# Graph-attention kernel on one Trainium2 core: a new schedule for the counting stage

## The reference

```python
x = x + gat(layernorm(x))             # 8 heads of 64
# per head h:
Wx = x @ Ws[h] + Wb[h]
s  = leaky_relu(Wx[dst] @ a_w[h,:64] + Wx[src] @ a_w[h,64:] + a_b[h], 0.2)
alpha = segment_softmax(s, dst)
out_h = segment_sum(alpha[:, None] * Wx[src], dst)
# then: a mixture of 16 experts (one chosen for all nodes), a graph
# convolution over the same edges with self loops, a mixture of 8 experts per node
```

## Time and profile before

| what | value |
|---|---|
| median of 3 runs | 553.72 us (551.4 to 556.36) |
| the profiled execution | 548.52 us, span 546.8 us |
| merge of pair 159, the last (end of the counting) | at 135.21 us of the span |
| TensorE busy over the span | 487.1 us (89%) |
| VectorE busy | 437.4 us (80%) |
| ScalarE busy | 343.9 us (63%) |
| GpSimd busy | 69.6 us (13%) |

### The profile page before, as it was taken

How to read it: one execution, slowest core, us unless ns; L and a number is a source line. 1 busy time by engine, 2 the same in 40 slices (tenths; PEclk the granted TensorE clock), 3 DMA queues, 4 the chain that set the end, 5 groups by cost and what they waited for, 6 DMA issues and landing times.

```text
span 546.8 us, 11526 instructions
## 1 busy us (share of the span) xinstructions
PE 487.1 (89%) x4388; PEld 356.0 (65%) x4389; DVE 437.4 (80%) x908; ACT 343.9 (63%) x659; POOL 69.6 (13%) x85
## 2 busy tenths in 40 slices
PE   0979999986689999999899889988899999999995
PEld 0756666664688888888677644544466587776662
DVE  8767777664999999995898778995787787887871
ACT  5366666657899999984665643344444558856820
POOL 3000000000000000000000020123334420321232
PEclk9989999998799999999999999999999999999998
DMA  6970000002011111102000069000001118966111
GB/s 153 354 258 1 1 2 1 2 2 100 2 50 50 50 50 49 50 4 78 1 1 0 2 221 337 1 0 2 3 21 42 59 60 298 373 237 215 62 54 54
DMA packets 25253, 45.11 MB, mean 82 GB/s; under 512 B 6962, under 2 KB 6998, under 8 KB 25197
## 3 DMA queue, kind: packets, MB, share of 16 engines
q1 hardware_dynamic: 23212, 39.16, 21.0%
q0 software_dynamic: 1952, 5.18, 2.6%
q10 hardware_dynamic: 32, 0.01, 0.0%
HBM read 33.23 MB, written 11.95 MB: 83 GB/s over the span
## 4 chain that ended last, share of the span: by engine, by line
PE 52%; DVE 33%; issue 8%; ACT 4%; DMA 2%; POOL 1%; ACTq 0%; SPq 0%; POOLq 0%; DVEq 0%
PE bank L1442 8%; PE bank L1832 6%; PE bank L1708 6%; DVE work L1125 4%; PE bank L1516 4%; PE bank L1468 4%; PE bank L1509 4%; PE bank L1803 3%; PE bank L1420 3%; PE bank L1611 3%; PE bank L1624 3%; DVE rings L1125 2%; DVE big L1235 2%; DVE st L887 2%; DVE work L1030 1%
## 5 line engine op out<-in xcount | busy, mean ns | idle before, releaser
L1611 PE MATMUL bank<-big,work 128*128 128x130 f16 x1080 | 67.4, 224 | 8.4 <-DVE work L1125 8.4
L1611 PEld LDWEIGHTS bank<-big,work 128*128 128x128 f16 x1080 | 64.3, 100 | 10.4 <-DVE work L1125 4.9
L1509 PE MATMUL bank<-big 128*128 128x180 f16 x320 | 58.1, 267 | 4.2 <-DVE big L988 4.2
L988 DVE TENSOR_TENSOR big<-mid 128x1024 f16<-128x1024 f16 (+1 forms) x88 | 59.8, 734 | 0.1
L685 ACT ACTIVATE mid<-aux,small 128x1280 f16<-128x1280 f32 x36 | 47.3, 1349 | 0.7 <-DVE work L1125 0.3
L1624 PE MATMUL bank<-big,mid 128*128 128x260 f16 x400 | 47.1, 275 | 0.1
L1708 PE MATMUL bank<-mid 128*128 128x512 f16 x200 | 47.2, 378 | 0.0
L586 ACT ACTIVATE mid<-bank 128x180 f32 x80 | 26.5, 331 | 28.9 <-PE bank L1516 28.1
L1624 PEld LDWEIGHTS bank<-big,mid 128*128 128x128 f16 x400 | 38.2, 96 | 7.5 <-issue 0.3
L1468 PE MATMUL bank<-big,rings 128*128 128x512 f16 x120 | 42.7, 378 | 0.1
L1509 PEld LDWEIGHTS bank<-big 128*128 128x128 f16 x320 | 35.6, 118 | 8.8 <-DVE big L988 5.9
(11 more groups left out here) (325 smaller groups left out, 1126.3 us busy)
## 6 DMA issues: line engine op xcount, KB each, us to landing
big<-in_L_ffn_W SPq DMA_DIRECT2D x10, 1024.0 KB, 9.0
mid<-in_L_ffn_W SPq DMA_DIRECT2D x6, 1024.0 KB, 14.4
xperm_scratch<-work SPq DMA_DIRECT2D x1, 5753.0 KB, 20.3
aux<-thr_scratch SPq DMA_DIRECT2D x8, 640.0 KB, 3.8
aux<-xperm_scratch SPq DMA_DIRECT2D x8, 523.0 KB, 4.3
row<-in_x SPq DMA_DIRECT2D x1, 2304.0 KB
aux<-in_L_gnn_Ws SPq DMA_DIRECT2D x4, 256.0 KB, 4.6
work<-in_L_gnn_W SPq DMA_DIRECT2D x1, 1024.0 KB, 6.6
```

The costliest lines, as they stand in the source:

```text
L988: return V.tensor_tensor(out.rearrange("p c (v two) -> p c v two", two=2), values.rearrange("p (v two) -> p v two", two=2).unsqueeze(1).to ...
L1509: mm(count_bank(base, k)[:, 0:RW], L_ring[:, slot, k * CH + j, :], R_ring[:, slot, k * CH + j, :], start=j == 0, stop=False)
L1611: ins = mm(acc_region(h, t), weighted[i % NC][:, t * P:(t + 1) * P], VP[:, s, part, h, :, :].rearrange("p b f -> p (b f)"), start=False, s ...
```

## The change

The schedule constants are new: 12 pairs a tile, first linear piece at pair 16, one piece a pair. The zeroing of C and C2 is split into halves: VectorE and ScalarE do one each, GpSimd two. The targets load before the sources, under semaphores of their own; four tiles of x load before the other six; the zero fill of a scratch tensor waits until all of x is there. The eight products on zeros are gone, all four W0 transposes come ahead of the tables' wait, ScalarE rounds W0 ahead of the pairs, tile 0's statistics stand in `pair_tables`. `scores` stands ahead of the last batch, `exponents` inside it, the threshold rows are copied by VectorE behind it, into another buffer.

```diff
-WARM = 8
-STEP = 10
-STATS_H = {(8 + STEP * t) // HALF: t for t in range(T)}
-SCALE_H = {(16 + STEP * t) // HALF: t for t in range(T)}
-LOW_H = {(24 + STEP * t) // HALF: t for t in range(T)}
-SQRT_P = {6 + STEP * t: t for t in range(T)}
-NORM_P = {15 + STEP * t: t for t in range(T)}
-ROWS_P = {17 + STEP * t: t for t in range(T)}
-COPY_P = {18 + STEP * t: t for t in range(T)}
-LIN_SLOTS = ((0,), (1,), (2,), (3,), (4, 5), (6,), (7,), (8, 9), (10,), (11,))
-LIN_P = {24 + STEP * t + i: (t, js) for t in range(T) for i, js in enumerate(LIN_SLOTS)}
-EVAC_P = {24 + STEP * (t + 1): t for t in range(T)}
-SCORES_H = max(EVAC_P) // HALF + 1
-EXPONENTS_H = SCORES_H + 2
-B_CS = SCORES_H // 2 + 1
-B_EXP = B_CS + 1
+STEP = 12
+FIRST_LIN = 16
+LIN_AT = [FIRST_LIN + STEP * t for t in range(T)]
+STATS_H = {(LIN_AT[t] - 16) // HALF: t for t in range(1, T)}
+SCALE_H = {(LIN_AT[t] - 12) // HALF: t for t in range(1, T)}
+LOW_H = {LIN_AT[t] // HALF: t for t in range(T)}
+SQRT_P = {LIN_AT[t] - 14: t for t in range(T)}
+NORM_P = {LIN_AT[t] - 10: t for t in range(T)}
+ROWS_P = {LIN_AT[t] - 9: t for t in range(T)}
+COPY_P = {LIN_AT[t] - 8: t for t in range(T)}
+LIN_P = {LIN_AT[t] + j: (t, j) for t in range(T) for j in range(STEP)}
+EVAC_P = {LIN_AT[t] + STEP: t for t in range(T)}
+XT0 = 4
...
+        half_words = T * NP // 4
...
-        thrT, _ = carve(work, 0, [NP])
+        thrT, _ = carve(rings, 0, [NP])
...
+            for n, (i_d, i_sb, name) in enumerate(((dst_d, dst_i, "ld_dst"), (src_d, src_i, "ld_src"))):
+                sp.wait_ge(sem("pads"), n + 1)
...
+            sp.dma_start(x[:, 0:XT0, :], x_d[0:XT0 * P, :].rearrange("(t p) d -> p t d", p=P)).then_inc(sem("ld_x0"), 16)
...
-            sp.dma_start(x[:, 0:T - 1, :], x_d[0:(T - 1) * P, :].rearrange("(t p) d -> p t d", p=P)).then_inc(sem("ld_x"), 16)
+            sp.dma_start(x[:, XT0:T - 1, :], x_d[XT0 * P:(T - 1) * P, :].rearrange("(t p) d -> p t d", p=P)).then_inc(sem("ld_x"), 16)
...
+            sp.wait_ge(sem("ld_x0"), 16)
+            sp.wait_ge(sem("ld_x"), 32)
             sp.wait_ge(sem("zero_set"), 1)
...
+            nc.gpsimd.memset(C2_words[:, half_words:2 * half_words], 0.0).then_inc(sem("C_zeroed"), 1)
+            nc.gpsimd.memset(C_words[:, half_words:2 * half_words], 0.0).then_inc(sem("C_zeroed"), 1)
...
             spread_a()
+            a.wait_ge(sem("ld_w0"), 16 * K)
+            act(W016[:, 0, :, :], W0.rearrange("p k h f -> p k (h f)"), ACT.Copy, scale=WS).then_inc(sem("weight_hi"), 1)
             lo_table(0)
...
-                    if b == B_EXP and k % 2 == 0:
-                        exponential(k // 2)
-                    if b == B_EXP + 1 and k == 1:
+                    if b == NB - 1 and 1 <= k <= 4:
+                        exponential(k - 1)
+                    if b == NB - 1 and k == 5:
...
-            V.memset(C2, 0.0).then_inc(sem("C_zeroed"), 1)
-            v.wait_ge(sem("ld_edges"), 64)
+            V.memset(C2_words[:, 0:half_words], 0.0).then_inc(sem("C_zeroed"), 1)
+            v.wait_ge(sem("ld_dst"), 32)
...
+                if beside:
+                    beside()
                 v.wait_ge(sem("table_psum"), p + 1)
...
                 for q in range(4):
+                    if q == 2:
+                        exponents()
...
+            def threshold_rows():
+                for i, n in enumerate((4, 4, 2)):
+                    v.wait_ge(sem("thrT_psum"), i + 1)
+                    V.tensor_copy(thrT[0:H, i * 512:i * 512 + n * P], bank[3 + i][0:H, 0:n * P]).then_inc(sem("thrT_ready"), 1)
+
+            def first_stats():
+                v.wait_ge(sem("ld_x0"), 16)
+                ln_stats(0, x[:, 0, :])
+
+            pair_tables(0, first_stats)
+            for b in range(NB):
+                if b == NB - 1:
                     scores()
                     last_onehots(b)
+                    threshold_rows()
...
                 else:
                     first_onehots()
-                    passes()
-                if b == 2:
+                    ln_scale(0)
...
             def count(base, slot, k):
                 pe.wait_ge(sem("onehots"), base + (k + 1))
+                if isinstance(base, int) and base == 0 and k < 3:
+                    pe.wait_ge(sem("w0T_ready"), (1, 2, K)[k])
...
-                if k == 2 and b == B_CS:
+                if k == 2 and b == NB - 2:
                     thresholds()
...
-            w0_T(0)
-            w0_T(1)
-            pe.wait_ge(sem("zero16_set"), 1)
-            for _ in range(WARM):
-                mm(bank[5][:, 0:400], zero16[:, 0:P], zero16[:, 0:400], start=True, stop=True)
+            for k in range(K):
+                w0_T(k)
```

More of the change, by code:

```diff
@@ L160, in gnn_ffn_kernel @@
         C2, o = carve(big, 9984, [T, NP], F16)
+        C_words, _ = carve(mid, 0, [T * NP // 2])
+        C2_words, _ = carve(big, 9984, [T * NP // 2])
+        half_words = T * NP // 4
         raw_at = free0 + T * H * FE
@@ L322, in count_bank, with w0_bank @@
             return bank[(0, 1, 7)[(base + k) % 3]] if isinstance(base, int) else bank[k % 2]
+        def w0_bank(k):
+            return bank[(0, 1, 6, 7)[k]]
         def gw_bank(k):
@@ L342, in _ @@
         def _(sp):
-            sp.wait_ge(sem("pads"), 2)
             full = (NG - 1) * RE
-            for i_d, i_sb in ((src_d, src_i), (dst_d, dst_i)):
-                sp.dma_start(i_sb[0:NG - 1, :], i_d[0:full].rearrange("(g e) -> g e", e=RE)).then_inc(sem("ld_edges"), 16)
-                sp.dma_start(i_sb[NG - 1:NG, 0:GLAST], i_d[full:EDGES].rearrange("(g e) -> g e", g=1)).then_inc(sem("ld_edges"), 16)
+            for n, (i_d, i_sb, name) in enumerate(((dst_d, dst_i, "ld_dst"), (src_d, src_i, "ld_src"))):
+                sp.wait_ge(sem("pads"), n + 1)
+                sp.dma_start(i_sb[0:NG - 1, :], i_d[0:full].rearrange("(g e) -> g e", e=RE)).then_inc(sem(name), 16)
+                sp.dma_start(i_sb[NG - 1:NG, 0:GLAST], i_d[full:EDGES].rearrange("(g e) -> g e", g=1)).then_inc(sem(name), 16)
             for k in range(K):
                 sp.dma_start(W0[:, k, :, :], Ws_d[:, k * P:(k + 1) * P, :].rearrange("h p f -> p h f")).then_inc(sem("ld_w0"), 16)
-            sp.dma_start(Wb_bc, Wb_d.partition_broadcast(P)).then_inc(sem("ld_x"), 16)
-            sp.dma_start(ab_bc, ab_d.partition_broadcast(P)).then_inc(sem("ld_x"), 16)
+            sp.dma_start(x[:, 0:XT0, :], x_d[0:XT0 * P, :].rearrange("(t p) d -> p t d", p=P)).then_inc(sem("ld_x0"), 16)
+            sp.dma_start(Wb_bc, Wb_d.partition_broadcast(P)).then_inc(sem("ld_w1"), 16)
+            sp.dma_start(ab_bc, ab_d.partition_broadcast(P)).then_inc(sem("ld_w1"), 16)
             sp.wait_ge(sem("pads"), 3)
-            sp.dma_start(x[:, 0:T - 1, :], x_d[0:(T - 1) * P, :].rearrange("(t p) d -> p t d", p=P)).then_inc(sem("ld_x"), 16)
+            sp.dma_start(x[:, XT0:T - 1, :], x_d[XT0 * P:(T - 1) * P, :].rearrange("(t p) d -> p t d", p=P)).then_inc(sem("ld_x"), 16)
             sp.dma_start(x[0:LAST, T - 1, :], x_d[(T - 1) * P:NODES, :]).then_inc(sem("ld_x"), 16)
@@ L655, in _ @@
                     act(cb16[0:64, :], bank[5][0:64, K * 2 * H:(K + 1) * 2 * H], ACT.Copy, scale=WS)
-                    a.wait_ge(sem("ld_x"), 64)
+                    a.wait_ge(sem("ld_w1"), 128)
                     act(Wb16[0:64, :], Wb_bc[0:64, :, :].rearrange("p h f -> p (h f)"), ACT.Copy, scale=WS).then_inc(sem("weight_hi"), 1)
[L658 to L661, removed]
             n = a.value_load(npass[0:1, 0:1], min_val=1, max_val=MAXPASS)
@@ L926, in _ @@
             V.tensor_tensor(both[gp, :], nwin[gp, 0:1], nwin[gp, 1:2], ALU.add).then_inc(sem("n_ready"), 1)
+            V.tensor_copy(dst16[gp, :], dst_i[gp, :])
+            v.wait_ge(sem("ld_src"), 32)
             link(V.tensor_scalar(hi_i[gp, :], src_i[gp, :], 7, None, ALU.logical_shift_right))
@@ L959, in passes, with pair_tables @@
                 V.tensor_copy(npass[0:1, :], npass_f[0:1, :]).then_inc(sem("npass_ready"), 1)
-            def pair_tables(p):
+            def pair_tables(p, beside=None):
                 V.tensor_tensor(end_[gp, :], begin[gp, :], nwin[gp, :], ALU.add)
@@ L1051, in _ @@
                         if u in STATS_H:
+                            if STATS_H[u] == XT0:
+                                v.wait_ge(sem("ld_x"), 32)
                             ln_stats(STATS_H[u], x[:, STATS_H[u], :])
@@ L1064, in _ @@
                                            ALU.mult, ALU.subtract).then_inc(sem("weight_lo"), 1)
+                if b == 1:
+                    passes()
                     v.wait_ge(sem("weight_hi"), 2)
@@ L1171, in _ @@
             V.tensor_tensor(mean, mean, bank[1][:, 0:K], ALU.add).then_inc(sem("mean_ready"), 1)
[L1172 removed]
+            v.wait_ge(sem("ld_w1"), 128)
             v.wait_ge(sem("gate"), 1)
@@ L1522, in w0_T @@
             def w0_T(k):
-                transposes(W0[:, k, :, :].rearrange("p h f -> p (h f)"), bank[k], "w0T_psum")
```

(13 more changed lines are left out.)

27 lines of the change are left out of this document (5 added, 22 removed).

## The result

| what | before | after |
|---|---|---|
| median of four runs | 552.89 us | 566.62 us (565.18 to 567.92) |
| ratio, 95% interval | | 1.0266 [1.0232, 1.03] |
| the profiled execution | 548.52 us | 565.18 us |
| merge of pair 8 | 30.58 | 34.09 |
| merge of pair 16 | 35.64 | 40.71 |

What follows compares the result with a forecast made beforehand. TensorE was taken to set the pace beside linear work, ScalarE's round trip elsewhere. From 548.5 us: start -2.7, fewer bare pairs and old stalls -9.6, new stalls +18.8, 555.0; plus 5.2 for the median and clock, 561; range 549 to 573.

Steps and rivals of the forecast that it cites:

- the late root: Linear part: square roots issued two pairs ahead of their half stall TensorE 2.1 us, nine times, 18.8 us in all.
- signs named ahead: Trace signs of being right: nine VectorE waits of some 4 us, nine TensorE waits of about 2.1, tiles 9.7 us apart.
- signs of being wrong: Stalls under 1 us, 7.6 us tiles, count(0) after 20 us, half-rate fp32 pieces, or first mask waiting for the threshold load.
- the start: Up to pair 8: split zeroing and earlier target loads gain 2.7 us, pair 8 at 27.9; bounds 3.7 us and 0.
- pairs 16 to 136: Linear part: ten tiles of 7.59 us plus eight stalls of 2.1 us, 92.7 us, pair 136 at 127.8.
- half of one: Clock allowance: half of one half-clock stretch, some 1.5 us each, added for nine idle stretches, taking 560.2 to 561 us.
- The clock rival: Start or stalls: TensorE falls to half clock without zero products or behind stalls, 567 to 580 us; chance 0.20.
- second half: Linear part: TensorE's clock falls behind several of the 2.1 us stalls, 1.5 us each, up to 13 us.
- The rival's first half: Start: without zero products TensorE may stay at 1.2 GHz until the fp32 pieces are over, some 6 us.
- the end: Pairs 136 to 159: 13.9 us instead of 14.8, pair 159 at 141.7, 6.5 us later than before.
- The threshold rows: After the last one-hots: ready about 11.7 us after pair 143, hidden by 1.9 us; without that cover up to 2 us.
- In sum: Whole kernel: +6.5 us on the profiled 548.5 us, 555.0 us; 560.2 in medians, 561 with the clock allowance.

Runs made afterwards that it cites:

- e1: Changed kernel with the square roots of tiles 1 to 9 moved six pairs earlier (eight pairs of lead): 546.37 us, ratio 0.9868 to the kernel before.
- e4: Kernel before, with only its square roots moved, to two pairs ahead of the half holding ln_scale, all ten tiles: 568.45 us, ratio 1.0295.
- e5: Changed kernel with the square roots of tiles 1 to 9 two pairs earlier (four pairs of lead): 553.7 us, ratio 1.0053.
- e2: Changed kernel with GpSimd's two zeroings held until VectorE has made its picks, the last small table operations: 565.21 us, ratio 1.0234.
- e3: Changed kernel with both edits: roots six pairs earlier, and GpSimd's zeroing held until VectorE's picks: 540.35 us, ratio 0.9762.
- e6: Changed kernel with roots six pairs earlier and no zeroing on GpSimd; VectorE zeroes all of C2, ScalarE all of C: 544.85 us, ratio 0.9869.
- e8: e3 with the eight products on zeros put back between the W0 transposes and the tables' wait: 540.13 us, ratio 0.9806.
- e9: Changed kernel with zeroing behind the picks and the old steps (ten pairs a tile, first linear piece at pair 24): 544.08 us, ratio 0.9865.
- e10: e3 with three quarters of the small fp32 products left out (weights_of and score_bias issue one of four): 538.11 us in one round, ratio 0.9763.

## Why the prediction came out as it did

**Right: the late root, its places and its size.** It was read from two dictionaries and five rows: nine stalls, the first the longest (2.12 us), at u = 4, 7, ..., 28. Priced at 2.1 us each; measured 1.96 by the spacing of the counts. The difference is reciprocal to remainder: 0.28 us in place of 0.39, because the row taken was a case in which the remainder started later. e1 takes the stalls away, e4 makes them in the old kernel, e5 has half of e1's lead and gets the price of the chain. Of the signs named ahead, TensorE's nine waits and VectorE's came, with tiles 9.8 to 10.1 us apart (9.7 forecast) where the clock held; so did one of the signs of being wrong, count(0) later than 20 us.

**Wrong: the start.** The step that failed is "GpSimd's two halves of 3200 words ... end at about 12.6; they are needed at count(0), about 6 us later, which hides them". Their length was even shorter than forecast (5.5 us for 6.5, ending at 11.5) and nobody waited for the result; but the instructions themselves shut out a VectorE operation on the chain that sets the start. Cost: pair 0 at 23.30 where it could be 17.33 (e2). That e2's edit alone brings it back is shown; that a shared port is the reason is argued, from the rule that follows. The Trainium skill, SBUF — State Buffer, section "Who interferes with whom", has it: VectorE and GpSimd share a port pair that one of them holds for its whole instruction, `tensor_scalar` is among the forms that can need it, `tensor_reduce` is not, and a `tensor_tensor` collides only with a GpSimd operation that reads SBUF. By that rule, the traces agree: the `tensor_scalar` stood until 11.5, to the end of both zeroings; in e2 and e3 the first one-hots, tensor-tensor operations, ran beside the end of the second zeroing at full speed. The row before the change could not show it: there GpSimd had nothing to do while that chain ran (its last operation began at 5.79, the chain at 7.71).

**Too low: pairs 16 to 136.** Predicted 92.7 us, measured 97.06. The stalls gave 15.6 (eight of 1.95) in place of 16.8. A tile without stall takes 8.0 us, not 7.59 (e1: 56.04 to 63.92 and 63.92 to 72.03 from merge to merge); the sum had left out the small gaps at the batch ends and ahead of the transposes. In e1 pairs 16 to 136 take 78.95 us, 3 us more than the 75.9 of the sum. And two stretches at half clock behind stalls took 1.2 to 1.3 us each: the forecast had half of one. These rows of the changed kernel answer to the earlier trace rows:

```profile
122.00:124.00 2.00, 2.00 (x11) 1.02 (x11) 2.00 (x4) 1.11 (x4) 0.00 (x0) 0.52 0.00 0
124.00:126.00 2.00, 2.00 (x14) 1.45 (x13) 0.52 (x1) 1.35 (x3) 0.00 (x0) 0.63 0.00 0
```

The clock rival was right mainly in its second half. In the linear part the three traces with full stalls (after, e2, e4) have one to three such drops each; e1, e3, e6, e8 and e9 have none, nor has e5 with its 0.7 us waits. e10 has one right behind pair 16, where its first pairs had been at half rate just before. The rival's first half, clock lost at the start, came in another form: not at count(0) but from pair 5 on, 3.4 us more at half rate than before. e8 shows that putting the zero products back does not remove it; what does cause it stays open.

**Too high: the end.** Predicted 13.9 us from pair 136 to 159, measured 12.34. The threshold copies off ScalarE and no clock drop there probably gave more than taken; no run takes the end apart. But 1.2 us of it comes back: ScalarE's table load (150.08 to 151.36) now stands between the last merges and the last two copies, which is why the copy of pair 159 is 16.1 us later and its merge only 14.9. The threshold rows were in time, as forecast.

**In sum,** the start was 6.2 us too low at pair 8 (34.09 against 27.9) and 5.6 us at pair 16 (40.71 against 35.1), the linear part 4.4 us. The end gave 1.6 back up to the merge of pair 159; 1.2 us were lost again at its copy and 0.5 us behind it. So against the profiled executions the sum was 10.2 us too low (555.0 against 565.2). That it was only 5.6 by the medians is luck: the 5.2 us by which the median of before lay over its profiled execution was carried over, and after the change it was 1.4 us; the 0.8 us added for the clock make up the rest. A single profiled execution is one draw out of a few microseconds.

**What beats both kernels:** e3, 540.35 us, ratio 0.9762 [0.9716, 0.9808]: the change, with its roots eight pairs ahead of the half that needs them and GpSimd held back until the picks.

## What to carry to other kernels

In a schedule written out by hand, check each hand-over between engines against how far each of them runs ahead. VectorE can work some 12 pairs ahead of TensorE, but a wait for something that ScalarE issues only two pairs ahead pulls it back, and everything behind the wait in its queue comes along. The price here is the chain from the producer to the work queued behind the wait (2.62 us), less what TensorE still has to do in that time (0.66 us at a lead of two pairs, 0.55 us more for each further pair), once for each occurrence. And before GpSimd gets work "for free", look at what VectorE runs in that time, not only at when the result is needed.

## What the runs showed of the hardware

- A GpSimd memset of 3200 words a partition (2.75 us) kept a VectorE `tensor_scalar` of 4 words from finishing for 5.90 us, through two such memsets in a row; the second one got in first although VectorE had been waiting since 5.62. In e2 a `tensor_scalar` of one word (0.15 us) and the first 16-bit `tensor_tensor` one-hots beside the second memset lost nothing.
- GpSimd's memset is as fast as VectorE's (2.75 against 2.73 us for 3200 words); the 523-word row had suggested 3.2 us.
- In the linear part, stalls of 1.8 to 2.3 us in TensorE's stream were followed one to three times a trace by 3.4 us at 1.2 GHz (6.8 us once), the stalls of up to 0.7 us in e5 never.
- By the end of the table products and 16 fp32 transposes TensorE was at 2.4 GHz in e8 (0.17 us for 400 columns right behind them, against 0.33 us behind eight transposes before). Not in every trace: in e1 and e6 the merge of pair 0 took 0.51 us, in the six others without zero products 0.31 to 0.33.
